# Expert blocks of 64 instead of 128 rows, as paired half-width products, with all low parts on VectorE

## The reference

```python
gate_logits = h2 @ Wg                                  # 625 x 8
w, sel = jax.lax.top_k(gate_logits, 1)
combine = zeros.at[arange(n)[:, None], sel].add(softmax(w))   # weight 1 at one expert
hid = relu(einsum('nd,edf->enf', h2, W1) + b1[:, None, :])    # 768 -> 3072
y = einsum('enf,efd->end', hid, W2) + b2[:, None, :]          # 3072 -> 768
out = x + einsum('ne,end->nd', combine, y)
```

## Time and profile before

| what | value |
|---|---|
| median of three runs | 1215.29 us (1214.89 to 1217.29) |
| the profiled execution's own time | 1210.92 us |
| its span | 1208.9 us |
| TensorE, busy share of the span | 88% |
| VectorE, ScalarE, GpSimd | 62%, 46%, 28% |
| expert stage, first expert product to last | 725.0 to 1201.9 us |

### The profile page before, as it was taken

The page is one execution under the profiler, slowest core; times in us unless marked ns, Lnnn a source line. Parts: engine busy times, 40 slices in busy tenths (PEclk is TensorE's granted clock), DMA queues, the critical chain, the costliest instruction groups (busy, mean ns, idle before and its releaser), DMA issues.

```text
span 1208.9 us, 19245 instructions
## 1 busy us (share of the span) xinstructions
PE 1059.0 (88%) x6178; PEld 660.8 (55%) x6179; DVE 752.7 (62%) x1289; ACT 558.7 (46%) x740; POOL 340.1 (28%) x184
## 2 busy tenths in 40 slices
PE   5989778999889759989989308999999999999997
PEld 3555467646656546556768204555555555555554
DVE  7677678783545863449966428793114989879611
ACT  2676557303131234238843027772114778778511
POOL 3100000290003322116001327652001656566400
PEclk9999889999989979989999658999999999999999
DMA  8920200022401440020000389995002999999500
GB/s 302 370 74 1 104 1 1 1 105 77 79 1 64 79 79 1 1 101 2 2 2 1 81 210 387 373 360 215 13 26 66 356 353 398 359 385 368 209 13 29
DMA packets 98379, 170.63 MB, mean 141 GB/s; under 512 B 38612, under 2 KB 38692, under 8 KB 98331
## 3 DMA queue, kind: packets, MB, share of 16 engines
q1 hardware_dynamic: 88138, 145.33, 34.6%
q0 software_dynamic: 6016, 16.80, 4.5%
q10 hardware_dynamic: 4176, 7.87, 2.1%
HBM read 153.19 MB, written 18.79 MB: 142 GB/s over the span
## 4 chain that ended last, share of the span: by engine, by line
PE 66%; DVE 16%; issue 7%; ACT 4%; DMA 2%; DVEq 2%; POOL 1%; POOLq 0%; ACTq 0%; SPq 0%
PE psum L1333 30%; PE psum L1532 14%; PE psum L1553 13%; DVE area L1274 4%; PE psum L1370 2%; PE psum L1322 2%; PE psum L1541 2%; DMA sorted_tokens<-area,smalls 2%; DVE smalls L923 1%; PE psum L1449 1%; DVE low L935 1%; DVE area L1179 1%; PE psum L1528 1%; DVE low L1039 1%; DVE low L1040 1%
## 5 line engine op out<-in xcount | busy, mean ns | idle before, releaser
L1333 PE MATMUL psum<-area,low 128*125 128x256 f16 (+2 forms) x1080 | 251.7, 395 | 21.2 <-DVE low L1118 10.9
L1274 DVE TENSOR_TENSOR area<-low,area 128x1536 f16<-128x1536 f32 x96 | 223.1, 2366 | 19.2 <-ACT area L852 19.1
L637 POOL TENSOR_TENSOR area<-low,area 128x1536 f16<-128x1536 f32 x48 | 184.5, 3843 | 156.7 <-ACT area L852 156.5
L852 ACT ACTIVATE area<-low 128x1536 f16<-128x1536 f32 x144 | 209.8, 1482 | 36.5 <-DMA low<-in_L_ffn_W_dram 29.8
L1532 PE MATMUL psum<-area,low 128*128 128x512 f16 x972 | 221.4, 382 | 0.0
L1553 PE MATMUL psum<-area,low 128*128 128x384 f16 x1296 | 217.9, 326 | 0.6 <-issue 0.3
L1333 PEld LDWEIGHTS psum<-area,low 128*125 128x125 f16 (+1 forms) x1080 | 151.9, 152 | 116.0 <-issue 65.6
L1553 PEld LDWEIGHTS psum<-area,low 128*128 128x128 f16 x1296 | 126.4, 98 | 80.2 <-issue 1.6
L1333 PE MATMUL psum<-area 125*128 125x64 f16 (+9 forms) x1076 | 145.4, 287 | 16.3 <-DVE area L1260 8.0
L1532 PEld LDWEIGHTS psum<-area,low 128*128 128x128 f16 x972 | 95.7, 98 | 114.6 <-issue 4.3
L1333 PEld LDWEIGHTS psum<-area 125*128 125x128 f16 (+3 forms) x1076 | 94.1, 128 | 51.2 <-issue 14.1
(11 more groups left out here) (205 smaller groups left out, 1295.5 us busy)
## 6 DMA issues: line engine op xcount, KB each, us to landing
low<-in_L_ffn_W_dram SPq DMA_DIRECT2D x144, 768.0 KB, 7.1
area<-in_L_gnn_W_dram SPq DMA_DIRECT2D x2, 3072.0 KB, 11.9
area<-in_L_gnn_Wr_dram SPq DMA_DIRECT2D x2, 3072.0 KB, 16.1
sorted_tokens<-area POOLq DMA_DIRECT2D x3, 1792.0 KB, 16.5
sorted_totals<-area POOLq DMA_DIRECT2D x3, 1792.0 KB, 28.7
low<-sorted_tokens ACTq DMA_DIRECT2D x11, 384.0 KB, 3.2
low<-sorted_totals ACTq DMA_DIRECT2D x9, 384.0 KB, 3.7
area<-in_L_ffn_Wv_dram SPq DMA_DIRECT2D x6, 384.0 KB, 6.3
```

The source lines that it names most:

```text
L637: pool.tensor_tensor(low_, raw_view(u), high_, ALU.subtract).then_inc(pool_low_ok, 1)
L852: act.activation(unit_parts(u)[0], raw_view(u), ACT.Copy).then_inc(high_ok, 1)
L1274: dve.tensor_tensor(low_, raw_view(u), high_, ALU.subtract).then_inc(dve_low_ok, 1)
L1333: ins = pe.matmul(place(name)[0:parts, at:at + w], left(q), right(q)[:, at:at + w], start=(q == 0), stop=(q == k - 1))
```

## The change

Blocks have 64 rows (BR = 64), so an expert's rows are padded to a multiple of 64, and up to 17 blocks are possible instead of 12. The six chunks are taken as three pairs (C2 = 3).

A first product now makes two chunks at once: for the same 64 tokens, one matmul writes the product with the even chunk of W1 into the output partitions 0 to 63, and the next the product with the odd chunk into the partitions 64 to 127 of the same bank. The stationary operand has 64 columns in each. A second product writes output columns 0 to 383 of the 64 rows into partitions 0 to 63 and columns 384 to 767 into partitions 64 to 127. The relu, the turning and the splitting still work on 128 partitions, on three tiles a block instead of six. Hidden tiles, turned tiles and their banks are no longer shared between chunks: there are three of each. The bias matmul of a pair takes its stationary operand from `picked`, a copy that ScalarE makes once a block (`pick_bias`).

VectorE makes the low parts of all 24 units, GpSimd none. The conversions go in six slices of four units. One slice (AHEAD = 1) is made for the next expert at the end of the block before it; in an expert's first block the others stand around the relu steps as `OWN` says. The last slice of W2 stands before the last inner low part.

The output is sent as half rows: 128 half rows of 384 values for 64 rows, with two numbers per row in `sorted_ids`. The residual rows and the numbers are loaded by two DMAs each. The next tokens are loaded as soon as TensorE has turned the present ones.

```diff
-    BR = 128
-    NB = T + E - 1
+    BR = 64
+    NB = (N + E * (BR - 1)) // BR
+    C2, HD = C // 2, D // 2
...
-        AHEAD, PER_STEP = 3, U // (C + 2)
+        AHEAD, PER_SLICE = 1, 4
+        OWN = (((1,), "first"), ((2,), "second"), ((3, 4), "third"), ((5,), None))
...
                 with eng.If(is_first > 0):
-                    for s_ in range(SPLIT):
-                        block_steps(b, e, s_)
-                        slice_(convert, a, b, s_ + AHEAD)
+                    for slices, what in OWN:
+                        for k in slices:
+                            slice_(convert, a, b, k)
+                        if what:
+                            block_steps(b, what)
...
+                block_steps(b, "last")
                 with eng.If(new_next > 0):
-                    for s_ in range(SPLIT, C + 2):
-                        block_steps(b, e, s_)
-                        slice_(convert, a + 1, b + 1, s_ - SPLIT)
...
+                    slice_(convert, a + 1, b + 1, 0)
+                block_steps(b, "end")
...
             def low_part(a, b, u):
-                if u not in POOL_UNITS:
-                    high_, low_ = unit_parts(u)
-                    dve.wait_ge(high_ok, a * U + (u + 1))
-                    dve.tensor_tensor(low_, raw_view(u), high_, ALU.subtract).then_inc(dve_low_ok, 1)
+                high_, low_ = unit_parts(u)
+                dve.wait_ge(high_ok, a * U + (u + 1))
+                dve.tensor_tensor(low_, raw_view(u), high_, ALU.subtract).then_inc(low_ok, 1)
...
                     for k in range(KD):
                         for x_, w_ in PARTS:
-                            ins = pe.matmul(psum[:, (c % 2) * BANK:(c % 2 + 1) * BANK], ht[x_][:, k, :],
-                                            w1_s[c][w_][:, k, :], start=False,
-                                            stop=(k == KD - 1 and x_ == 1))
+                            for half in range(2):
+                                ins = pe.matmul(psum[half * BR:(half + 1) * BR, p * BANK:(p + 1) * BANK], ht[x_][:, k, :],
+                                                w1_s[2 * p + half][w_][:, k, :], start=False,
+                                                stop=(k == KD - 1 and x_ == 1))
...
-                    for j in range(CK):
-                        for x_, w_ in PARTS:
-                            for q in range(2):
-                                ins = pe.matmul(psum[:, (4 + q) * BANK:(4 + q) * BANK + D // 2],
-                                                hidT[c % 2][x_][:, j, :],
-                                                w2_s[c][w_][:, j, q * D // 2:(q + 1) * D // 2],
...
+                    for half in range(2):
+                        for j in range(CK):
+                            for x_, w_ in PARTS:
+                                for q in range(2):
+                                    ins = pe.matmul(psum[q * BR:(q + 1) * BR, 6 * BANK:6 * BANK + HD],
+                                                    hidT[p][x_][:, j, half * BR:(half + 1) * BR],
+                                                    w2_s[2 * p + half][w_][:, j, q * HD:(q + 1) * HD],
...
-                for s_ in range(C + 2):
-                    if s_ < C:
+                for s_ in range(C2 + 2):
+                    if s_ < C2:
                         first_product(s_)
```

More of the change, by code:

```diff
@@ L206, in gnn_moe_kernel @@
         assert W1W == W2W and 2 * W1W + D <= XW and 2 * W1W <= CWD
-        y_o = low[:, TW + 2 * W1W:TW + 2 * W1W + D]
-        xt = T_[:, 0:D]
-        turned = v3(xt, KD)
+        y_o = low[:, TW + 2 * W1W:TW + 2 * W1W + HD]
+        xt = T_[0:BR, 0:D]
         at_t = [D]
+        B1_AT = TW - CW // 2 - E * C // 2
         def carve(n):
             at_t[0] += n
-            assert at_t[0] <= 4400
+            assert at_t[0] <= B1_AT
             return T_[:, at_t[0] - n:at_t[0]]
-        ht = [v3(carve(D // 2).bitcast(F16), KD) for _ in range(2)]
-        hid = [carve(CW) for _ in range(2)]
-        hidT = [[v3(carve(CW // 2).bitcast(F16), CK) for _ in range(2)] for _ in range(2)]
-        UNITS = [(w, c, q) for s in range(1, C + 2) for w, c in ((1, s - 1), (2, s - 2)) if 0 <= c < C
-                 for q in range(2)]
+        turned = v3(carve(KD * BR), KD)
+        ht = [v3(carve(KD * BR // 2).bitcast(F16), KD) for _ in range(2)]
+        hid = [carve(CW) for _ in range(C2)]
+        hidT = [[v3(carve(CW // 2).bitcast(F16), CK) for _ in range(2)] for _ in range(C2)]
+        UNITS = [(w, 2 * p + half, q) for s in range(1, C2 + 2) for w, p in ((1, s - 1), (2, s - 2)) if 0 <= p < C2
+                 for half in range(2) for q in range(2)]
         U = len(UNITS)
@@ L260, in gnn_moe_kernel @@
         pos_i = small(P, T, dt=U32)
-        token_id = small(P, T, dt=I32)
+        token_id = small(P, T, 2, dt=I32)
         ids = small(128, 1, dt=U32)
-        tab = small(1, 4, NB, dt=I32)
+        tab_at = TW + 2 * W1W + HD
+        tab = v3(low[0:1, tab_at:tab_at + 4 * (NB + 1)].bitcast(I32), 4)
+        picked = v3(low[0:112, tab_at + 4 * (NB + 1):tab_at + 4 * (NB + 1) + C * BR // 2].bitcast(F16), C)
+        assert 2 * W1W + HD + 4 * (NB + 1) + C * BR // 2 <= XW
         nblocks = small(1, 1, dt=I32)
@@ L656, in _ @@
                 send_rows()
-                with pool.If(is_first > 0):
-                    for u in POOL_UNITS:
-                        if u >= early:
-                            low_unit(a, u)
             blocks = pool.value_load(nblocks[0:1, 0:1], min_val=1, max_val=NB)
@@ L839, in _ @@
             act.wait_ge(routed, 1)
-            act.sem_inc(hid_cp, 2)
+            act.sem_inc(hid_cp, C2)
             def high_part(a, b, u):
@@ L1228, in _ @@
             link(dve.tensor_scalar(nblk, number, 0.0, None, ALU.is_gt))
-            for q in range(1, T):
+            for q in range(1, -(-N // BR)):
                 link(dve.scalar_tensor_tensor(out=nblk, in0=number, scalar=float(q * BR), in1=nblk,
@@ L1290, in first_tokens, with inner_low, block_steps @@
                 tokens_low(b)
-            def block_steps(b, e, s_):
-                if s_ == 3:
-                    turn_in(b + 1)
-                if 1 <= s_ <= C:
-                    c = s_ - 1
-                    dve.wait_ge(hidhi_ok, b * C + (c + 1))
-                    dve.tensor_tensor(hidT[c % 2][1], v3(psum[:, (2 + c % 2) * BANK:(3 + c % 2) * BANK], CK),
-                                      hidT[c % 2][0], ALU.subtract).then_inc(hid_relu, 1)
-                    if c == C - 1:
-                        tokens_low(b + 1)
-            def block_end(b):
-                dve.wait_ge(hid_used, b * C + 2 * C)
-                dve.wait_ge(rest_in, b * 32 + 32)
-                dve.tensor_tensor(v3(y_o, 2), v3(psum[:, 4 * BANK:6 * BANK], 2)[:, :, 0:D // 2], v3(y_o, 2),
-                                  ALU.add).then_inc(y_cp, 1)
+            def inner_low(b, p):
+                dve.wait_ge(hidhi_ok, b * C2 + (p + 1))
+                dve.tensor_tensor(hidT[p][1], v3(psum[:, (C2 + p) * BANK:(C2 + p + 1) * BANK], CK),
+                                  hidT[p][0], ALU.subtract).then_inc(hid_relu, 1)
+            def block_steps(b, what):
+                if what == "second":
+                    inner_low(b, 0)
+                    turn_in(b + 1)
+                if what == "third":
+                    inner_low(b, 1)
+                    tokens_low(b + 1)
+                if what == "last":
+                    inner_low(b, 2)
+                if what == "end":
+                    dve.wait_ge(hid_used, b * C2 + 2 * C2)
+                    dve.wait_ge(rest_in, b * 64 + 64)
+                    dve.tensor_tensor(y_o, psum[:, 6 * BANK:6 * BANK + HD], y_o, ALU.add).then_inc(y_cp, 1)
             dve.sem_inc(y_cp, 1)
-            expert_blocks(dve, low_part, first_tokens, block_steps, block_end)
+            expert_blocks(dve, low_part, first_tokens, block_steps)
         @block.tensor
```

175 lines of the change are left out of this document (79 added, 96 removed).

## The result

The changed kernel takes 1221.77 us in the median of five runs (1220.14 to 1224.57), the kernel before 1214.89 us in its five. The ratio is 1.0076 with a 95% interval of 1.0054 to 1.0097: slower by 0.8%, clear of noise. The profiled execution took 1223.64 us with a span of 1221.9 us, 13.0 us longer than the span before.

What follows compares the result with a forecast made beforehand. TensorE bounds compute-only blocks; with new experts, transfer comes within 2 us. Block ends, 3 us for the clock, tail and routing gave span 1220.5, own time 1222.5 and, 4.4 us higher, a median of 1227 us; range 1206 to 1285.

Steps and rivals of the forecast that it cites:

- expert 0's block ends: First block of the expert stage: its end was predicted at 774 us instead of 783.0.
- N: TensorE's part of a 64-row block: 26.5 us (25.8 to 27.5) with pairs overlapping, against 51.3 for 128 rows.
- expert 3's block, behind such blocks: New expert's block after compute-only blocks, with six units waiting in the buffers: 49.5 us (46.5 to 52).
- expert 7's first block: New expert's block after a compute-only block, predicted like expert 3's: 49.5 us.
- clock, behind new experts: Lower TensorE clock after idle gaps: 1.5 us added at each of two places where a compute-only block follows a new expert.
- The overlap of the pairs: In TensorE's products, two matmuls on different output halves cost what one does: 25.8 us a block, 49.4 without overlap.
- The drains: TensorE's ten changes a block between full-width matmuls and pairs: 0 to 1.6 us, taken as 0.7.
- Rival 3: VectorE's low parts stay at 2.37 us despite GpSimd leaving; 64 us an expert, about 1305 us in all; chance 0.05.
- some 25 us of idle TensorE: Expected sign in each block with a new expert: TensorE idle some 25 us, waiting for VectorE's low parts.
- The loop's top: Four table reads at the start of each block, counted as 2.8 us in VectorE's 48.2 us for a new expert.
- The offset of 4.4 us from profiled run to median: Last step from the profiled run's own time, 1222.5 us, to the predicted median, 1227 us.
- Rival 2: Faster side: no drains, new experts at bare transfer's pace, no clock loss; about 1209 us; chance 0.28 including up to the forecast.

Runs made afterwards that it cites:

- experiment 1: The changed kernel with each product's matmuls ordered all of one output half, then all of the other, so no neighbouring pairs: 1420.7 us in one run.
- Experiment 2: Three variants of the changed kernel: less weight transfer 1218.8 us, low part a copy instead of a subtraction 1208.8 us, both 1174.3 us.
- experiment 8: Unused expert-number read removed from VectorE's and ScalarE's loop top: 1221.84 us on the changed kernel; 1201.77 us on the earlier kernel with GpSimd making only five late low parts.
- experiment 7: The changed kernel told there is one block less, so the last block's rows are not computed: 1195.02 us, ratio 0.9852 to the kernel before.
- the same four traces: The changed kernel as is (1221.77 us), with one block less (1195.02), without an unused table read (1221.84), and with two slices converted ahead (1225.87).
- experiment 4: The changed kernel with a pair's bias added by two matmuls of 64 columns instead of one of 128: 1216.55 us, ratio 1.0020 to the kernel before.
- experiment 3: The changed kernel with every third low part made by GpSimd again: 1270.5 us, ratio 1.0469 to the kernel before.

## Why the prediction was right

The direction, the size (1227 us predicted, 1221.8 measured) and the mechanism held; some terms of the sum did not, and they cancelled. The steps, against the marks in the trace:

| step | predicted | in the trace |
|---|---|---|
| expert 0's block ends | 774 | 767.9 |
| expert 1's first block ends | 824 | 819.1 |
| a block that only computes (N) | 26.5 (25.8 to 27.5) | 27.2 |
| expert 3's block, behind such blocks | 49.5 | 51.3 |
| experts 4 and 6, first blocks | 51, 51 | 51.3, 51.0 |
| expert 7's first block | 49.5 | 51.3 |
| clock, behind new experts | +3 | 0 there |
| last product to the end | 7 - 0.5 | 7.3 |
| span | 1220.5 | 1221.9 |

The overlap of the pairs. Full overlap was taken and is what happens; apart, the same matmuls cost 45.6 us a block (experiment 1), not the 49.4 of the upper bound. The drains were taken as 0.7 us a block and are 1.4: 27.2 less the 25.8 of the row arithmetic. The Trainium skill (TensorEngine Tiling (Array Packing), Key Properties) says that changing the mode drains TensorE; the trace agrees in direction, with 0.09 to 0.15 us at each change where a full wait for the last product would be about 0.17 (a bias lasts 0.39 us in its record, and before the next product started 0.22 us behind it). The block that the prediction worked out by that rule, 27.4 us, is nearer to the 27.2 measured than the 26.5 it took. With the Trainium skill's next statement there, that different tiles can load and multiply in parallel, the trace agrees too: 36 matmuls in 4.00 us against 18 in 3.89. That column tiling gives up the fast weight load stands in the Trainium skill under Restrictions on the same page, not where the prediction has it. A load lasts 110 ns for the 64 columns of a second product and lasted 98 ns for 128, and at 4.00 us for 36 matmuls it costs nothing that the trace shows.

VectorE alone on the low parts. The median of 1.75 us was read rightly as the undisturbed time: in the changed kernel all 144 lie between 1746 and 1760 ns.

```profile
L1272 DVE TENSOR_TENSOR area<-low,area x144: 1746/1753/1760, 713.5 to 1153.6; 128x1536 f16<-128x1536 f32 x144
```

Rival 3 is out by this row.

Where the halved work went. Experiment 2 shows the two limits that were expected close under TensorE, one by one, and the block at 51 us. The mark of some 25 us of idle TensorE in such a block was missed: it is 18 to 19 us, since TensorE's work takes 32 to 33 us there, at a granted clock of 0.80 to 0.83.

The mis-sized terms. The loop's top in VectorE's sum was 2.8 us; it costs 0.7 in the trace, and taking a read out of it changes nothing (experiment 8). In its place stand waits that I priced too low: VectorE idles 1.70, 1.46 and 1.04 us for ScalarE, which at 939.8 had waited for a product of 6.85 us at the lower clock. That is why behind blocks that only compute it is 51.3 us and not 49.5. The trace of experiment 7, where this block has the same code, bears it out in part:

```profile
933.14 0.61 PE L1527 MATMUL psum<-low 112*128 112x512 f16 x1 [4.35 <-DVE area L1272]
933.68 5.19 PE L1532 MATMUL psum<-area,low 128*64 128x512 f16 x36
```
```profile
963.84 0.69 DVE L1292 TENSOR_TENSOR low<-psum,low 128x512 f16<-128x512 f32 x1 [0.24 <-ACT low L854]
```

Behind the same gap the product takes 5.19 us instead of 6.85. VectorE's wait of 1.70 us is gone and the one of 1.46 is 0.24, and the block lasts 48.8 us at a granted clock of 0.86. So in these two traces 2.5 us of this block hang on how long the clock stays at its lower level. Expert 7's block, predicted alike, stays at 50.7 to 51.3 us in the same four traces, so 49.5 was too low for it with any clock seen. The prediction had this cost in another place and miscounted the places: it added 1.5 us at two blocks that only compute and follow a new expert. There are three, behind experts 1, 6 and 7, and all three last 27.2 us at a granted clock of 1.00.

Expert 0's end is early by 6 us, and 4.6 us of it is the start of the stage at 720.4 instead of 725.0. This start varies by 9 us between traces, so luck has a part in it. Another part may belong to the change: it lay between 719.7 and 724.1 in the nine traces with blocks of 64 rows and no low parts on GpSimd, and between 724.6 and 729.0 in the four with blocks of 128. No run separated the two. N was too low by 5 us over seven blocks and the blocks of experts 3 and 7 by 3.6 us, and these cancelled the 6 us and the 3 us for the clock. A span right within 1.4 us is thus better than the terms deserve. The offset of 4.4 us from profiled run to median failed by itself: the profiled run of the change lay 1.9 us above its median, so the predicted time is 5 us high.

Rival 2, the fast side, lacked two things that it counted on: the changes between full width and halves cost 1.4 us a block, and the buffers do fill and empty. From 927.9 to 1081.6 SyncE waited 66 times for VectorE's low parts before it could refill a buffer, and ScalarE 32 times for a unit still on its way, so that neither limit is reached bare. Halving the bias alone brings the kernel to 0.2% above the one before (experiment 4), so 5 to 7 of this side's 18 us hung on one instruction.

## What to carry to other kernels

Halving an engine's work helps only in the stretches that it bounds: here six of nine blocks had two other limits within 2 us. The sign was then decided by the count of blocks: one expert of 82 rows cost a block of 27.2 us more, twice the 13 us that the kernel lost. Before making blocks smaller, count the blocks for the real row counts, and multiply by what a block costs where nothing hides it. When one part of a change alone is a gain (the low parts on one engine, or GpSimd kept away from where its neighbour is awaited), try it without the rest. The first gave 0.6% here and the second 1.0%, while the whole change lost 0.8%. And before reading 2 us out of two profiles, look at the granted clock of the two stretches.

## What the runs showed of the hardware

Taken apart, 36 matmuls of 512 columns (18 on one half of the output partitions, then 18 on the other) took 7.05 us, less than 36 x 0.216 = 7.78 us; the 48 of 384 columns took 7.30 instead of 7.80. In the single records of the first product the matmuls of the second half begin at 864.45, beside one of the first half at 864.44, and some three run side by side at this place; the others are 216 ns apart. This was not tested further.

GpSimd's low parts and VectorE's disturb each other. VectorE's take 1.75 us undisturbed and up to 4.7 us beside GpSimd. GpSimd's take 3.1 to 4.7 us in the kernel before and up to 7.6 in experiment 3; one with no work of VectorE beside it, at 778.3 in experiment 3, took 3.09. And a share of 8 in 24 given back to GpSimd cost 6.6 us of VectorE's busy time in expert 3's block, although VectorE made a third fewer.
